# Router's first layer issued a step earlier, some copies on VectorE, small work moved

## What is computed

```python
def routed_ffn(x):              # f1, f3: 512 tokens at a time
    h = relu(x @ rW1 + rb1); h = relu(h @ rW2 + rb2)      # 128 -> 512 -> 512
    scales = softmax(h @ rW3 + rb3)                       # 8 experts
    top_scales, top_experts = top_k(scales, 2)
    pos = exclusive_cumsum(onehot)  # place in the expert; kept while pos < capacity
    y = relu(dispatched @ eW1) @ eW2                      # per expert
    return sum(top_scales * gathered(y))
# r2: retention, 16 heads of 8 channels
def relative(src):              # f4, f6
    x = layernorm(src); q, k, v = x @ wq, x @ wk, x @ wv
    att = softmax((q @ k.T + shifted(q @ (pe @ wp).T)) * scale)
    src = src + (att @ v) @ wo
    x2 = layernorm(src); sel = sigmoid(x2 @ sel_w)
    gate = top 4 of 32 of sel
    return src + sum_e gate_e * (relu(x2 @ keys_e) @ values_e)
# a5: the same softmax attention without positions
```

## Time and profile before

| | us |
|---|---|
| median of 3 runs | 3286.7 (3285.94 to 3289.89) |
| the profiled execution: its time | 3284.24 |
| its span on the core | 3282.4 |
| busy PE | 2909.0 (89%), 21536 instructions |
| busy PE weight loads | 2356.4 (72%) |
| busy DVE | 2005.9 (61%) |
| busy ACT | 2049.9 (62%) |
| busy POOL | 1992.1 (61%) |
| mean granted clock of PE | 0.952 of full speed |

### The profile page before, as it was taken

One profiled execution on the slowest core, in us unless ns is written; L12 is line 12 of the kernel. 1 busy time (PEld: TensorE's weight loads), 2 busy tenths in 40 slices (PEclk: granted clock), 3 DMA queues, 4 the chain that ended last, 5 costly groups with the idle time before them and its releaser, 6 DMA issues. The chain is left out here.

```text
span 3282.4 us, 64177 instructions
## 1 busy us (share of the span) xinstructions
PE 2909.0 (89%) x21536; PEld 2356.4 (72%) x21536; DVE 2005.9 (61%) x4546; ACT 2049.9 (62%) x6021; POOL 1992.1 (61%) x2415
## 2 busy tenths in 40 slices
PE   5899678799969999997999979996899999979998
PEld 4778556577858877885788856664678777858886
DVE  4544466445437777775555548886577777745554
ACT  2223233232239999996544449997799999944443
POOL 3223554232238788784999942222778878759998
PEclk9999889799979999998999989998899999989999
DMA  3000355000012122122555533332212211145554
GB/s 105 1 1 1 91 115 112 7 1 1 1 37 50 40 50 50 40 50 66 193 192 193 192 96 78 78 78 48 59 40 50 50 40 43 37 167 187 190 193 168
DMA packets 145535, 261.88 MB, mean 80 GB/s; under 512 B 13402, under 2 KB 118106, under 8 KB 122298
## 3 DMA queue, kind: packets, MB, share of 16 engines
q1 hardware_dynamic: 145210, 257.78, 27.1%
HBM read 204.06 MB, written 53.67 MB: 79 GB/s over the span
## 5 line engine op out<-in xcount | busy, mean ns | idle before, releaser
L2230 POOL TENSOR_TENSOR f6m_ht_lo<-f6m_ht,f6m_ht_hi 128x512 fp32r<-128x512 f32 x256 | 330.4, 1309 | 33.2 <-ACT f6m_ht_hi L2175 23.5
L2230 POOL TENSOR_TENSOR f4m_ht_lo<-f4m_ht,f4m_ht_hi 128x512 fp32r<-128x512 f32 x256 | 331.4, 1313 | 31.3 <-ACT f4m_ht_hi L2175 21.7
L2175 ACT ACTIVATE f6m_ht_hi<-f6m_ht 128x512 fp32r<-128x512 f32 x256 | 161.5, 632 | 191.5 <-DVE f6m_ht L2210 191.4
L2175 ACT ACTIVATE f4m_ht_hi<-f4m_ht 128x512 fp32r<-128x512 f32 x256 | 161.5, 632 | 190.6 <-DVE f4m_ht L2210 190.2
L2210 DVE SCALAR_TENSOR_TENSOR f6m_ht<-f6m_hr,f6m_gate 128x512 f32<-128x512 f32 x256 | 176.2, 691 | 168.4 <-PE f6m_hr L2106 160.8
L2210 DVE SCALAR_TENSOR_TENSOR f4m_ht<-f4m_hr,f4m_gate 128x512 f32<-128x512 f32 x256 | 176.3, 691 | 167.7 <-PE f4m_hr L2106 159.5
L1702 ACT ACTIVATE a_pr<-a_sr,a_nm 128x256 f32<-128x256 f32 x512 | 258.4, 589 | 10.6 <-DVE a_nm L1831 10.5
L1958 POOL TENSOR_TENSOR f4a_rr<-f4a_tmp 128x256 f32<-128x256 f32 x256 | 189.6, 741 | 107.5 <-DVE f4a_tmp L1839 106.8
L1958 POOL TENSOR_TENSOR f6a_rr<-f6a_tmp 128x256 f32<-128x256 f32 x256 | 189.5, 741 | 107.2 <-DVE f6a_tmp L1839 106.5
L1702 ACT ACTIVATE f4a_pr<-f4a_sr,f4a_nm 128x256 f32<-128x256 f32 x512 | 241.0, 488 | 6.6 <-DVE f4a_nm L1831 6.6
L1702 ACT ACTIVATE f6a_pr<-f6a_sr,f6a_nm 128x256 f32<-128x256 f32 x512 | 240.9, 487 | 6.6 <-DVE f6a_nm L1831 6.6
(11 more groups left out here) (419 smaller groups left out, 9939.6 us busy)
## 6 DMA issues: line engine op xcount, KB each, us to landing
f4m_gate<-f4m_gates SPq DMA_DIRECT2D x64, 1024.0 KB, 4.6
f6m_gate<-f6m_gates SPq DMA_DIRECT2D x64, 1024.0 KB, 4.6
r_scratch<-r_parts SPq DMA_DIRECT2D x32, 192.0 KB, 2.2
all_qs<-r_scratch SPq DMA_DIRECT2D x16, 384.0 KB, 4.8
all_ks<-r_scratch SPq DMA_DIRECT2D x16, 384.0 KB, 6.6
f4a_scratch<-f4a_parts SPq DMA_DIRECT2D x32, 192.0 KB, 2.2
all_qs<-f4a_scratch SPq DMA_DIRECT2D x16, 384.0 KB, 5.1
all_ks<-f4a_scratch SPq DMA_DIRECT2D x16, 384.0 KB, 6.7
```

The costliest lines, as they stand in the source:

```text
L2175: nc.scalar.activation(ht_hi[:, n % RB, :], ht[:, n % RB, :], ACT.Copy).then_inc(hi_ready, 1)
L2230: nc.gpsimd.tensor_tensor(ht_lo[:, n % RB, :], ht[:, n % RB, :], ht_hi[:, n % RB, :], ALU.subtract)\
```

## The change

Three parts.
- In f1 and f3: layer1 of the next group goes from the start of its step to the end of the step ahead, between `turn_weights` and `logits`; `turn_x` goes ahead of the step's last outputs; `orders`, ACT, DVE and POOL follow that order. In `pick`, `max_index`, the copy, two comparisons and a sum become a memset, four `match_replace` and one comparison. DVE clears the padding after the first results of layer1 instead of ahead of the weights' lo halves.
- In f4a and f6a: DVE makes the copies of `take_turned` for m = 2, 6, 10, 14, so in slots 4, 8, 12 and 0; `x2t` goes from slot 11 to 12, `sel` from 13 to 14, both parts of `gate` to slot 15; the clearing and the split of the first step go from slot 4 to 8.
- In f4a, a5 and f6a: POOL's wait for the stage's loads goes from its start to the one operation that reads them (the bias in a5).

```diff
-        best, best_at = a.sb("best", [P, GT, 8]), a.sb("best_at", [P, GT, 8], U32)
+        best, left = a.sb("best", [P, GT, 8]), a.sb("left", [P, GT, E0])
...
@@ PE, routed_ffn @@
                 if s == 0:
                     turn_x(0)
+                    for m in range(KH):
+                        layer1(0, m)
...
-                if route:
-                    for m in range(KH):
-                        layer1(s, m)
                 if s % 2:
...
                     if route:
                         layer2(s, 2)
+                    if s < G - 1:
+                        turn_x(s + 1)
                     if expert:
                         output(q, e + 2)
...
                     if route:
                         layer2(s, 3)
+                    if s < G - 1:
+                        turn_x(s + 1)
                     if expert:
                         for n in range(4):
                             output(q, e + n)
                 if route:
                     partial(s)
-                if s < G - 1:
-                    turn_x(s + 1)
                 if given:
                     turn_weights(group)
+                if s < G - 1:
+                    for m in range(KH):
+                        layer1(s + 1, m)
                 if route:
                     logits(s)
...
@@ DVE, pick and mark @@
-                dve.wait_ge(best_step, g * 2 + 1)
+                dve.wait_ge(best_step, g * 3 + 1)
+                nc.vector.memset(best[:, :, 2:8], -1.0).then_inc(best_step, 1)
+                dve.wait_ge(best_step, g * 3 + 2)
                 nc.vector.memset(k.idle, 0.0)
                 for t in range(GT):
-                    last = nc.vector.max_index(best_at[:, t, :], best[:, t, :], sc[:, t, :])
+                    last = nc.vector.match_replace(left[:, t, :], best[:, t, :], sc[:, t, :], -1.0)
                 last.then_inc(best_step, 1)
...
+                nc.vector.tensor_scalar(mask[:, :, :], left[:, :, :], 0.0, None, ALU.is_lt).then_inc(mask_step, 1)
...
@@ DVE, start and loop of routed_ffn @@
-            for n, tile in enumerate([eos] + gts):
-                nc.vector.memset(tile[64:ROWS, :, :, :].rearrange("p b v c -> p (b v c)"), 0.0).then_inc(padded, 1)
...
-                if route:
-                    route_hidden(s, "h1", 1)
-                    route_hidden(s, "h1", 3)
+                if s == 0:
+                    route_hidden(0, "h1", 1)
+                    route_hidden(0, "h1", 3)
+                    for n, tile in enumerate([eos] + gts):
+                        nc.vector.memset(tile[64:ROWS, :, :, :].rearrange("p b v c -> p (b v c)"), 0.0).then_inc(padded, 1)
...
                 if given:
                     take_weights(group, 1)
                     take_weights(group, 3)
+                if s < G - 1:
+                    route_hidden(s + 1, "h1", 1)
+                    route_hidden(s + 1, "h1", 3)
...
@@ POOL, routed_ffn @@
             rest_of_x(0)
+            for m in range(KH):
+                rest_of_h1(0, m)
             for s in range(G + 1):
-                if s < G:
-                    for m in range(KH):
-                        rest_of_h1(s, m)
-                if s:
+                if s < G - 1:
+                    ln_root(s + 1)
+                if s and s % 2 == 0:
                     weigh(s - 1)
                 if s < G - 1:
-                    ln_root(s + 1)
                     rest_of_x(s + 1)
+                if s % 2:
+                    weigh(s - 1)
+                if s < G - 1:
+                    for m in range(KH):
+                        rest_of_h1(s + 1, m)
...
@@ softmax_attention @@
-        AT = {"xt": 8, "qk": 10, "x2t": 11, "sel": 13, "src": 0, "ln": 4} if rel else {"xt": 13, "qk": 15, "ln": 8}
+        AT = {"xt": 8, "qk": 10, "x2t": 12, "sel": 14, "src": 0, "ln": 4} if rel else {"xt": 13, "qk": 15, "ln": 8}
...
-            return rel or n % 2 == 1
+            return n % 4 != 2 if rel else n % 2 == 1
...
+            def clear():
                 nc.vector.memset(vm[:, :, :, :, :].rearrange("p a b c d -> p (a b c d)"), 0.0).then_inc(vm_zero, 1)
...
-                    if rel and n in (14, 15):
-                        gate(it, n - 14)
+                    if rel and n == 15:
+                        gate(it, 0)
+                        gate(it, 1)
...
+                    if rel and n == 8 and is_first(i):
+                        clear()
...
                     if not rel and n == 7:
+                        pool.wait_ge(loaded, LOADS)
...
             pool.wait_ge(k.loaded, k.loaded_count)
-            pool.wait_ge(loaded, LOADS)
             Pipeline.run(pool, step)
```

More of the change, by code:

```diff
@@ L152, in routed_ffn @@
             if route:
-                orders["rv"] += [("h2", (s, 1)), ("h2", (s, 3)), ("logits", s)]
-                if s < G - 1:
-                    orders["ra"].append(("x", s + 1))
+                orders["ra"] += [("h2", (s, 0)), ("h2", (s, 2))]
+                orders["rv"] += [("h2", (s, 1)), ("h2", (s, 3))]
+            if s < G - 1:
+                orders["ra"].append(("x", s + 1))
+            if route:
+                orders["ra"].append(("partial", s))
+            if s < G - 1:
+                orders["ra"] += [("h1", (s + 1, 0)), ("h1", (s + 1, 2))]
+                orders["rv"] += [("h1", (s + 1, 1)), ("h1", (s + 1, 3))]
+            if route:
+                orders["rv"].append(("logits", s))
             for ring, half in (("ea", 0), ("ev", 1)):
@@ L476, in _ @@
                     take_x(0)
+                    route_hidden(0, "h1", 0)
+                    route_hidden(0, "h1", 2)
                 if s == 1:
@@ L513, in _ @@
                         hidden(q, e + 3)
+                    if s < G - 1:
+                        take_x(s + 1)
+                    if expert:
                         output(q, e // 2)
@@ L521, in _ @@
                     take_weights(group, 2)
+                if s < G - 1:
+                    route_hidden(s + 1, "h1", 0)
+                    route_hidden(s + 1, "h1", 2)
                 if route:
@@ L588, in pick @@
                 last.then_inc(best_step, 1)
-                dve.wait_ge(best_step, g * 2 + 1)
+                dve.wait_ge(best_step, g * 3 + 1)
+                nc.vector.memset(best[:, :, 2:8], -1.0).then_inc(best_step, 1)
+                dve.wait_ge(best_step, g * 3 + 2)
                 nc.vector.memset(k.idle, 0.0)
                 for t in range(GT):
-                    last = nc.vector.max_index(best_at[:, t, :], best[:, t, :], sc[:, t, :])
+                    last = nc.vector.match_replace(left[:, t, :], best[:, t, :], sc[:, t, :], -1.0)
                 last.then_inc(best_step, 1)
-                dve.wait_ge(best_step, g * 2 + 2)
-                nc.vector.tensor_copy(best_f[:, :, :], best_at[:, :, 0:2]).then_inc(bestf, 1)
             def mark(g):
-                dve.wait_ge(bestf, g * 2 + 1)
-                for n in range(2):
-                    last = nc.vector.tensor_tensor(eq[:, :, n, :], k.iota8.unsqueeze(1).to_broadcast([P, GT, E0]),
-                                                   best_f[:, :, n:n + 1].to_broadcast([P, GT, E0]), ALU.is_equal)
-                last.then_inc(bestf, 1)
-                dve.wait_ge(bestf, g * 2 + 2)
-                nc.vector.tensor_tensor(mask[:, :, :], eq[:, :, 0, :], eq[:, :, 1, :], ALU.add).then_inc(mask_step, 1)
+                dve.wait_ge(best_step, g * 3 + 3)
+                nc.vector.tensor_scalar(mask[:, :, :], left[:, :, :], 0.0, None, ALU.is_lt).then_inc(mask_step, 1)
                 dve.wait_ge(mask_step, g + 1)
```

22 lines of the change are left out of this document (8 added, 14 removed).

## The result

The changed kernel takes 3240.1 us (median of 4 runs, 3238.95 to 3242.6), the kernel before, on the same chip, 3286.3 (3285.8 to 3289.89, 4 runs): a ratio of 0.9856, with a 95% interval of 0.9842 to 0.987. The profiled execution took 3240.78 with a span of 3239.0, so 43.5 less than that of before (3284.24); my sum was 46.3.

What follows compares the result with a forecast made beforehand. PE, busy 89% of the span, was taken as the bound. Savings 8.0 + 1.8 + 15.2 + 6 + 8.5 + 2.6 + 4.2 = 46.3 off 3284.24, plus 2.5 for the median, gave 3240; range 3224 to 3256, 8 in 10 3214 to 3264.

Steps and rivals of the forecast that it cites:

- Start of f1: With DVE's memsets behind layer1's results, layer1 starts at 16.4 instead of 24.41: 8.0 us saved.
- Router's steps: In f1 and f3, logits between layer1 and layer2 shorten each wait by 0.95: 7.6 us a stage, 15.2 together.
- the clock: In f1 and f3, shorter waits remove half of eight half-clock stretches, each costing some 1.5: 6 us, ends 0 and 12.
- The count: Routed steps: its mask comes some 2.8 us later, yet ready before PE's count; no cost taken, up to 1 a step possible.
- Starts of f4a, f6a, a5 and f3: POOL's later load waits save 4.4, 4.1 and 2.6 in f4a, f6a, a5; memsets gone from f3's start save 1.8.
- The collision that I took off: Starts of f4a and f6a: the memset, moved four slots on, meets POOL's next roots; 1.6 us deducted.
- Steady steps: Attention steps of f4a and f6a: DVE's later maxima eat nearly all gained; -0.14 a step, 2.1 a stage, 4.2 together.
- The -1.68 of slots 11 to 15: Steady attention steps: moving `x2t` and `sel` one slot and copies off ACT removes PE waits of 1.44 and 0.24.
- A: Steady attention steps: DVE's lateness is not felt, -1.68 a step counts in full, 50.4 instead of 4.2: 3194; chance 0.12.
- C: Attention, slots 15 to 5: DVE becomes the bound; 3304 at 2.0 a step, chance 0.06 slower; milder 3259 to 3283, 0.10.
- B: Routed stages give nothing in their steps, the count or POOL becoming the wait; 15.2 and 6 fall out: 3261; chance 0.14.
- D: Only the starts count, the chains in the steps being taken up by others: 20.9 saved, 3266; chance 0.04.

Runs made afterwards that it cites:

- e6: Changed kernel with the logits ahead of layer1 again in f1 and f3: 3261.5 us, ratio 0.9916 to the kernel before.
- e8: Changed kernel with the clearing and the first step's split moved on to slot 1 of the second step: 3243.9 us, ratio 0.9864.
- e10: Changed kernel with DVE's copies in slots 2, 6, 10, 14, POOL's splits ahead of its forms, clearing in the second step's slot 5: 3220.0 us, 0.979.
- e9: Changed kernel with POOL's splits of q and k (slots 1 and 3) ahead of its forms of the same slot: 3237.9 us, ratio 0.9846.
- e4: Changed kernel with all copies back on ACT, slots and gate as changed: 3237.6 us, ratio 0.9844.
- e12: Changed kernel with `x2t`, `sel` and gate back in slots 11, 13, 14 and 15, DVE's copies in slots 2, 6, 10, 14: 3244.8 us, 0.9869.
- e5: Changed kernel with DVE's copies in slots 2, 6, 10 and 14 instead of 4, 8, 12 and 0: 3220.8 us, ratio 0.9788.

## Why the prediction was right, and where not

**Forecast 3240, measured 3240.1.** The agreement of the whole is better than that of its terms, since two errors of opposite sign met.

*Start of f1*, 8.0: 7.4. The order of events was right; that POOL's 1.26 becomes 1.87 beside DVE's subtraction with two inputs in SBUF was not seen.

*Router's steps*, 7.6 a stage, and the clock 3 a stage: 10.8 and 14.1. The mechanism was right, by e6: with the logits back the waits are back. The waits' term was right in size too. PE's idle time in the two stages, from layer1's first product on, fell by 8.0 and 8.7; less the 0.9 of it at f3's start that is 15.8 against 15.2; a wait shrank by 1.2, but the logits cost PE more in their new place, and 0.9 (against e6) to 1.0 a step (against the kernel before) is left. Step s = 1, for which I took 1.9, gave 1.3 and 0.4. Undersized was the clock: PE's busy time fell by 2.8 and 7.2; less the 1.0 at f3's start that is 9.0 against 6. The price of a stretch, 1.5, was right by e6 (though full clock makes 25 products in such a window, not 31); its count was not, since six of eight went where I took half, and f3 lost one more, in its second step. The count is no wait anywhere in the list of waits, as taken.

*Starts of f4a, f6a, a5 and f3*: 4.5, 3.7, 2.6 and 1.8 against 4.4, 4.1, 2.6 and 1.8. The collision that I took off, 1.6, is there: 1.5 in f4a (1.68 for 0.20), and 2.1 in f6a (2.83 for 0.70), where 0.4 is missing. The rule weighed in the prediction, that of the Trainium skill, page "SBUF — State Buffer", section "Who interferes with whom", would have no memset hold GpSimd on this chip. The runs show otherwise for `clear` 28 times, on small roots and on a split; whether by the memset or by what stands behind it is open, as said under e8 and e10. Beside the 32-partition memsets of f1 and f3 the trace agrees with the page, 1.27 as without them. The same section has a DVE instruction with two SBUF inputs contend with GpSimd's reads, and there the trace agrees: 1.87 for 1.26 at 15.11.

*Steady steps*, 2.1 a stage gained: 0.7 and 1.4 lost. The chain of maxima, exponentials and scores was worked out rightly to some 0.15 us a slot, for a normal step -0.40 in place of -0.14. The step that failed is "POOL runs some 1.2 later in slots 0 to 8 and stays ahead of its use". It does for the scores. But its splits in slots 1 and 3 feed SP's transfers, and PE comes for the stacked keys 1.34 earlier behind the split than it did (11.94 for 13.28): the margin that hid a late transfer in five of thirteen steps was gone, and it cost 0.43 a step on average. e9, which gives it back (13.25), has one such wait in f4a in place of five, and none in f6a. I had followed the engines that wait for POOL and not the queue.

*ACT.* The -1.68 of slots 11 to 15 was one term, for the move of `x2t` and `sel` and for the copies. By e4 the move alone gives 0.91 there (11.47 before, 10.56 in e4), the copies the other 0.8; by e12 the copies alone give nothing. In the change they cost as much in slots 0 to 7 as they give, so that they are worth nothing where they stand (e4), and 17 us two slots earlier (e4 against e5).

*Rivals.* A (DVE's lateness not felt) is refuted by the slots 2 and 3, C (DVE as the bound) by DVE's 246 us in 300 with a step of 35.1. B and D are refuted by f1 and f3.

## What to carry to other kernels

When short work moves within a queue, ask of each consumer when it comes for its data, the transfers included: a stop of PE that goes away takes with it the margin of every transfer that is due behind it. A queue that is full over two slots isn't relieved by taking work out of a third; the order of its own instructions around the late one tells what helps. And independent work of PE put between the start and the end of another engine's chain can be worth more than its own time, where the clock falls after the wait that it shortens.
